# Decoder kernel, first attention stage: the key-partition scores of a group's four heads issued back to back in two ring places

## The reference

```
A0, causal self-attention, 16 heads of 16 values, 512 keys:
  q3, k3 = x @ wq, x @ wk                       # 3 numbers a head
  scores = (q3 . k3) * scale + (q3 . dir)(k3 . dir), masked above the diagonal
  out    = softmax(scores) @ v, then @ wo
X0, cross attention, 16 heads of 16, 1024 keys of the context:
  q = x @ Wq + bq; k, v = ctx @ Wk + bk, ctx @ Wv + bv
  out = softmax(clip(q . k / 4, +-10000)) @ v, then @ Wo + bo
```

## Time and profile before

| | us |
|---|---|
| median of 3 launches | 1334.27 (1333.01 to 1334.39) |
| the profiled execution, its own time | 1329.35 |
| its span, first to last instruction | 1327.6 |
| PE busy | 1193.6 (90%) |
| DVE busy | 742.4 (56%) |
| ACT busy | 556.9 (42%) |
| POOL busy | 89.6 (7%) |
| mean granted clock of TensorE | 0.956 of full speed |

### The profile page before, as it was taken

The page is one execution under the profiler, slowest core; times in us unless marked ns, Lnnn a source line. Parts: engine busy times, 40 slices in busy tenths (PEclk is TensorE's granted clock), DMA queues, the critical chain, the costliest instruction groups (busy, mean ns, idle before and its releaser), DMA issues.

```text
span 1327.6 us, 20645 instructions
## 1 busy us (share of the span) xinstructions
PE 1193.6 (90%) x7754; PEld 754.9 (57%) x7754; DVE 742.4 (56%) x1099; ACT 556.9 (42%) x1070; POOL 89.6 (7%) x127
## 2 busy tenths in 40 slices
PE   5999887899999986889599999999999999998887
PEld 3454444233332234778367777767777777777545
DVE  3346476888898845453256554655455554554322
ACT  1343332555555641221156663655334444453230
POOL 1112211000000003000000000000000000000120
PEclk9898877999999987999799999999999999999989
DMA  5010002000000002000242331223443333120000
GB/s 169 9 49 18 8 1 64 0 1 1 1 1 1 1 1 80 0 0 1 68 119 65 80 80 33 65 64 81 113 120 80 80 81 81 31 50 1 0 16 16
DMA packets 46917, 57.47 MB, mean 43 GB/s; under 512 B 12635, under 2 KB 25446, under 8 KB 46822
## 3 DMA queue, kind: packets, MB, share of 16 engines
q1 hardware_dynamic: 43062, 52.48, 16.3%
q10 hardware_dynamic: 3760, 3.67, 0.9%
HBM read 15.23 MB, written 3.15 MB: 14 GB/s over the span
## 4 chain that ended last, share of the span: by engine, by line
PE 79%; DVE 9%; issue 6%; ACT 3%; POOL 1%; DMA 1%; SPq 1%; POOLq 0%; ACTq 0%; DVEq 0%
PE p_unit L1531 21%; PE p_ring L1531 11%; PE p_ring L1632 9%; PE p_out L1655 8%; PE p_ring L1551 8%; PE p_ring L1598 7%; PE p_out L1621 6%; PE p_unit L1716 2%; PE p_ring L1576 2%; PE p_unit L1675 1%; DVE probT_b L1341 1%; PE p_ring L1590 1%; DVE stats L1244 1%; POOL m_z L1064 1%; PE p_ring L1569 1%
## 5 line engine op out<-in xcount | busy, mean ns | idle before, releaser
L1153 ACT ACTIVATE probT_b<-p_ring 128x512 f32<-128x512 f32 x144 | 84.5, 598 | 260.4 <-PE p_ring L1632 260.0
L1311 DVE TENSOR_REDUCE halves<-p_ring 128x2 f32<-128x1024 f32 x128 | 155.6, 1218 | 40.9 <-PE p_ring L1576 40.7
L1341 DVE COPY probT_b<-p_ring 128x512 f32<-128x512 f32 x112 | 77.4, 691 | 174.0 <-PE p_ring L1632 174.0
L1135 ACT ACTIVATE prob_a<-p_ring 128x1024 f32<-128x1024 f32 x128 | 130.7, 1023 | 93.8 <-PE p_ring L1598 93.8
L1293 DVE TENSOR_REDUCE nmax<-p_ring 128x2 f32<-128x1024 f32 (+1 forms) x128 | 155.9, 1218 | 23.5 <-PE p_ring L1551 23.5
L1121 ACT ACTIVATE prob_b<-p_ring,nmax 128x512 f32<-128x512 f32 (+1 forms) x192 | 158.7, 835 | 2.6 <-DVE nmax L1293 2.3
L1551 PE MATMUL p_ring<-stacks 128*128 128x512 f32 x512 | 150.8, 417 | 4.5 <-ACT prob_b L1121 4.5
L1632 PE MATMUL p_ring<-ident,prob_b 128*128 128x128 f32 x1024 | 134.6, 274 | 0.0
L1632 PEld LDWEIGHTS p_ring<-ident,prob_b 128*128 128x128 f32 x1024 | 115.8, 141 | 27.7 <-issue 25.8
L1598 PE MATMUL p_ring<-x_q,x_kq 32*128 32x512 f32 x512 | 126.5, 656 | 0.0
L1551 PEld LDWEIGHTS p_ring<-stacks 128*128 128x128 f32 x512 | 87.0, 190 | 17.0 <-ACT prob_b L1121 5.1
(11 more groups left out here) (201 smaller groups left out, 1658.6 us busy)
## 6 DMA issues: line engine op xcount, KB each, us to landing
stacks<-splitH_b SPq DMA_DIRECT2D x144, 128.0 KB, 2.4
stacks<-splitL_b SPq DMA_DIRECT2D x144, 128.0 KB, 2.4
a_st<-a_image SPq DMA_DIRECT2D x64, 32.0 KB, 1.8
ctx_raw<-in_ctx ACTq DMA_DIRECT2D x1, 1536.0 KB, 15.5
x<-in_x ACTq DMA_DIRECT2D x2, 512.0 KB, 5.2
k_words<-in_L_ffn_k SPq DMA_DIRECT2D x1, 1024.0 KB, 6.7
a_wq<-in_L_attn_Wq SPq DMA_DIRECT2D x1, 1024.0 KB, 6.2
a_wo<-in_L_attn_Wpost SPq DMA_DIRECT2D x1, 1024.0 KB, 9.3
```

What stands on the lines that cost most here:

```text
L1135: nc.scalar.activation(prob_place(key), slot_of("S2", key), ACT.Exp, accum_out=x0_sums[:, m:m + 1]).then_inc(done["E2"], 1)
L1311: nc.vector.tensor_reduce(to, src, AX.X, ALU.max, negate=True).then_inc(done["M1"], 1)
L1341: keep_turned(dve, key, lambda o, i: nc.vector.tensor_copy(o, i)).then_inc(done["VD"], 1)
```

## The change

`scored` is a new list of S2 items whose E2 is still to come. When it is empty and the next group's maxima are there, two S2 items (the two pairs of one block of keys, so all four heads) are added to the schedule at once, and both go into `scored`; in each iteration one E2 is taken from it. So the S2 of pair 1 is issued one iteration earlier, straight behind that of pair 0, and the ring's order becomes S2 S2 S1 S1 in place of S2 S1 S2 S1. Nothing else moves except what depends on it: the k and q units of X0 and the loads of A0's stacks wait for the last S2 of an earlier group, and come an iteration sooner. The remaining edits name the places of the operands by (batch, group) in place of a position in `PAIRS`; with `PAIRS` as it is they give the same places. The number of iterations and of instructions stays.

```diff
@@ paired_stream
-        if s < len(second) and age("UD", "mt", *second[s][:3]) >= 2:
-            it = second[s]
-            s += 1
-            sched.add("S2", *it)
+        if not scored and s < len(second) and age("UD", "mt", *second[s][:3]) >= 2:
+            for it in second[s:s + 2]:
+                sched.add("S2", *it)
+                scored.append(it)
+            s += 2
+        if scored:
+            it = scored.pop(0)
             sched.add("E2", *it)
             fresh.append(it)
@@ build_schedule
-    def used(n):
-        return [("S2", prob_items(PAIRS[n])[-1])] if n >= 0 else []
+    def used(L, n):
+        return [("S2", prob_items((L, n // 4, n % 4))[-1])] if n >= 0 else []
@@ block.tensor, "S1" of X0
-                        place = (G - 8) % HELD
+                        place = place_of_heads((L, b, g))
```

More of the change, by code:

```diff
@@ L153, in paired_stream @@
     heads = [list(c) for c in chains]
-    pending, owed, clean, adds, keep = [], [], [], [], []
+    pending, owed, clean, adds, keep, scored = [], [], [], [], [], []
     f = s = n = 0
@@ L170, in ready @@
         return item[0] <= n and all(a in sched.at for a in item[2])
-    while f < len(first) or s < len(second) or pending or owed or clean or adds or keep or any(heads):
+    while f < len(first) or s < len(second) or pending or owed or clean or adds or keep or scored or any(heads):
         while pending:
@@ L373, in a0_start @@
         for g in range(4):
-            out.append(step("DS", "A0", b, g, after=[UD("q", "A0", b)] + used(4 * b + g - HELD)))
+            out.append(step("DS", "A0", b, g, after=[UD("q", "A0", b)] + used("A0", 4 * b + g - HELD)))
         return out
@@ L381, in x0_keys @@
         n = 4 * b + g - HELD
-        return [unit("k", "X0", b, g, h, after=used(8 + n) if n >= 0 else []) for h in range(2)]
+        return [unit("k", "X0", b, g, h, after=used("X0", n)) for h in range(2)]
     def x0_queries(b, g):
         n = 4 * b + g - HELD
-        return [unit("q", "X0", b, g, after=[turned_x("A0", b)] + (used(8 + n) if n >= 0 else []))]
+        return [unit("q", "X0", b, g, after=[turned_x("A0", b)] + used("X0", n))]
     last_one = prob_items(PAIRS[-1])[-1]
@@ L773, in prob_place, with x0_back, place_of_heads @@
             return prob_a[:, prob_no[it] % NPT, :, :]
+        def x0_back(b, g):
+            n = 4 * b + g - HELD
+            return ("X0", n // 4, n % 4)
+        def place_of_heads(grp):
+            return (4 * grp[1] + grp[2]) % HELD
         def pair_back(grp, k):
@@ L950, in _ @@
                     if grp >= HELD:
-                        wait(sp, "S2", *prob_items(PAIRS[grp - HELD])[-1])
+                        wait(sp, "S2", *prob_items(("A0", (grp - HELD) // 4, (grp - HELD) % 4))[-1])
                     for which in range(2):
@@ L1036, in _ @@
                     if 4 * b + g >= HELD:
-                        wait(pool, "S1", *max_items(PAIRS[8 + 4 * b + g - HELD])[-1])
+                        wait(pool, "S1", *max_items(x0_back(b, g))[-1])
                     nc.gpsimd.tensor_copy(x0_kqF[:, place, part, :], x0_kq[:, place, part, :]).then_inc(done["KF"], 1)
@@ L1189, in _ @@
                         if 4 * b + g >= HELD:
-                            wait(act, "S2", *prob_items(PAIRS[8 + 4 * b + g - HELD])[-1])
+                            wait(act, "S2", *prob_items(x0_back(b, g))[-1])
                         if u[0] == "q":
@@ L1452, in _ @@
                             ins = nc.vector.tensor_tensor(a0_q2[:, G % 2, :], p_unit[:, :],
-                                                          a0_st[:, G % HELD, 1, :].bitcast(F32), ALU.add)
+                                                          a0_st[:, place_of_heads(grp), 1, :].bitcast(F32), ALU.add)
                         else:
                             ins = nc.vector.tensor_tensor(x0_q2[:, G % 2, :], p_unit[:, :],
-                                                          x0_kq[:, (G - 8) % HELD, 2, :], ALU.add)
+                                                          x0_kq[:, place_of_heads(grp), 2, :], ALU.add)
                     elif u[0] == "dt":
@@ L1560, in _ @@
                     if L == "A0":
-                        pe.wait_ge(a0_stacked[G % HELD], 16 * 8 * (G // HELD + 1))
+                        pe.wait_ge(a0_stacked[place_of_heads(key[:3])], 16 * 8 * ((4 * b + g) // HELD + 1))
                         w = 128 * (i + 1)
@@ L1564, in _ @@
                             r = 64 * pr + 32 * aa
-                            nc.tensor.matmul(o[:, aa, 0:w], a0_st[r:r + 17, G % HELD, 1, 128 * i:128 * i + 128],
-                                             a0_st[r:r + 17, G % HELD, 0, 0:w], start=True, stop=False,
+                            nc.tensor.matmul(o[:, aa, 0:w], a0_st[r:r + 17, place_of_heads(key[:3]), 1, 128 * i:128 * i + 128],
+                                             a0_st[r:r + 17, place_of_heads(key[:3]), 0, 0:w], start=True, stop=False,
                                              tile_position=(r, 0))
@@ L1590, in _ @@
                                 ins = nc.tensor.matmul(o[:, aa, at:at + T - 128 * c],
-                                                       a0_st[r:r + 17, G % HELD, 0, 128 * c:128 * c + 128],
+                                                       a0_st[r:r + 17, place_of_heads(key[:3]), 0, 128 * c:128 * c + 128],
                                                        a0_q2[r:r + 17, G % 2, 128 * c:T], start=True, stop=True,
```

## The result

The changed kernel takes 1351.91 us (median of 11 runs, 1339.91 to 1360.14), the kernel before in the same session 1333.01 us (11 runs, 1326.90 to 1338.54). The ratio is 1.0133 with a 95% interval of 1.0098 to 1.0167: slower by 13 to 22 us. Ratios are estimated over all launches but the slowest one of the changed kernel (1360.14), so a ratio can differ by some tenths of a per cent from the quotient of two medians, which is 1.0142 here. The forecast was 1344.7 in a range of 1334 to 1358, so the side and the range hold. The sizes of its terms don't.

What follows compares the result with a forecast made beforehand. TensorE held the chain for 79% of the span; PE and DVE were nearly full in X0, PE in A0. Terms 8.0 + 0.1 - 0.2 - 1.0 + 1.0 + 2.5 = 10.4 on the 1334.27 median gave 1344.7 us, range 1334 to 1358.

Steps and rivals of the forecast that it cites:

- the stall behind the q copy: X0 groups with units: ACT copies q ahead of the second E2, so PE idles 1.44 us before the next two S2.
- a change of more than 5 us ahead of 205 us: Sign named beforehand: a change this large in the trace there would show that the prediction has A0 wrong.
- A0, the step that failed: A0: copy stalls against 0.15 to 0.2 us saved per two S2; between minus 5 and plus 7, plus 1 taken.
- both S1 stand uncovered: X0 on PE: the two S1 cost 0.32 and 0.43 us; with 1.07 for two S2, 1.82 against 1.6 before.
- the wait of the first S1 for the M1 just before it: X0's new order: 1.88 us from M1 to M1 where it was 1.73, making 3.61 us per two S2.
- The clock: Five X0 stalls may halve PE's clock, costing 0 to 17 us; half the stalls at 1 us taken, plus 2.5.
- The rival of a falling clock: X0 stalls and iterations without units halve PE's clock: some 17 us instead of 2.5, 1359 us; chance 0.15.
- Number 1 to 7: X0 group, first to seventh M1, with k, k and q units: 16.8 us against 15.02, plus 1.8.
- Number 7 to 9 and 9 to 15: X0 group, seventh to ninth M1: 4.84 against 5.17, minus 0.3; ninth to fifteenth: 10.8 against 10.69, plus 0.1 to 0.2.
- The end of X0: Where no S1 is left, one S2 or PV is saved: minus 1.0 us, between minus 2 and 0.
- The sum: X0 8.0 + 0.1 - 0.2 - 1.0, A0 plus 1.0, clock plus 2.5: 10.4 us slower.
- Packing: Faster rival: X0's adjacent S2 save PE time, 9 us, 1325 us (chance 0.12); in full 27 us, 1307 us (0.03).

Runs made afterwards that it cites:

- A0 filled: Six more mask matmuls in every S1 of A0: added to the changed kernel 1346.0 us (1.0088), to the kernel before 1329.9 us (0.9994).
- taking it away alone: Kernel before with six more mask matmuls per A0 S1, and A0's two S1 pairs swapped, so S1 takes the preceding S2's rows: 1339.2 us (1.0050).
- taken away, in whole and in part: Changed kernel, S1 ahead of the two S2: 1360.7 us; changed kernel with six more mask matmuls per A0 S1, PV ahead of S1 in A0: 1344.1 us.
- copies behind E2: Changed kernel with ACT's copies of X0's k and q units behind the iteration's E2 instead of ahead of it: 1349.0 us (1.0103).
- couples in A0 only: Changed kernel issuing two S2 together only in A0, X0 one S2 an iteration as before: 1353.2 us (1.0163).
- couples and late copies in X0 only: Changed kernel with two S2 together only in X0, and ACT's copies of X0's k and q units behind E2: 1338.3 us (1.0022).
- couples in X0 only: Changed kernel issuing two S2 together only in X0, A0 as before: 1332.2 us (0.9991).

## Why the prediction came out as it did

That the change would cost, and that X0's groups would be longer by the stall behind the q copy, was right. That the total fell into the range was luck: X0 as a whole costs nothing, and A0, which was put at next to nothing, costs all of it. The prediction named the sign itself: a change of more than 5 us ahead of 205 us would show that it has A0 wrong, and X0 began 24.5 us late.

- **A0, the step that failed.** The prediction's sentence was that its "S2 is one pass and short, so PE gains little there", with bounds of minus 5 to plus 7 from copy stalls and a small gain a couple, and plus 1 taken. With A0 filled, X0 starts 11.1 us late (184.0 against 172.9), and 6.2 us of that is lost in five groups at full clock. Two terms stood in the working for X0 ("both S1 stand uncovered", and the wait of the first S1 for the M1 just before it), and neither was counted in A0. In X0 packing saves PE more than the uncovered S1 cost it: busy 158.8 us against 165.9 in the five groups, with DVE busy 85% of the time. In A0, where PE is busy 91% and DVE half of the time, PE's work grows, by 3.0 us in the five groups of the filled kernels, and 3.1 us of M1 waits come with it. That the lost cover costs is shown by taking it away alone. That the M1 waits cost is not: they were taken away, in whole and in part, and those groups stayed as long. What makes the rest of the 6.2 us stays open.
- **The clock.** I put it at plus 2.5 for stalls in X0. There it cost at most 0.7 us (one group of 36.6). It fell in A0, where the traced execution of the changed kernel was at half clock for 41 us on end from 103.9 us; with the filler the time is 5.9 us less by the medians, which is not clear of the noise. The rival of a falling clock had the wrong place: X0 is granted 0.99 from 276.1 to 456.3 us.
- **The stall behind the q copy.** Right: 1.35 us against 1.44, and every start from the first k unit to the second couple is within 0.1 us of the forecast, counted from the first S1 at 313.28, but for the S1 behind the first couple (6.58 against 7.05). It was not what sets the group, as the copies behind E2 show.
- **Number 1 to 7.** 16.08 us against 16.8. The first M1 comes 1.06 after its S1, not 0.61, since DVE is behind, which takes 0.45 off. The S1 behind the second couple starts inside it, so that M1 number 5 comes 13.58 after the first S1, not 13.82: 0.24. From number 5 to 7 it is 1.75 and 1.81, not 1.73 and 1.88: 0.05.
- **Number 7 to 9 and 9 to 15.** Minus 0.47 (forecast minus 0.3) and minus 0.03 (plus 0.1 to 0.2). A couple is 3.55 us, not 3.61, and was 3.56 before. So a group costs 0.57 instead of 1.6, and five such groups 2.9 instead of 8.0.
- **The end of X0.** Minus 2.7 (55.9 to 53.2) against minus 1.0, with bounds of minus 2 to 0: more than the bound. I counted one S2 or PV; which steps make the rest was not followed.
- **The sum.** X0 as run is near 0 where 6.9 was forecast (8.0, 0.1, minus 0.2, minus 1.0). A0 with its clock is 18.2 us by the medians (couples in A0 only, 1353.2 - 1335.0), 21.8 by the ratio and 24.5 by the trace, where 3.5 stood, the whole clock term counted in. The whole is 18.9 us by the medians, against 10.4.
- **Packing.** The eight records do run beside one another in 1.14 us. That rival missed for the reason given: half of the gain was taken before, because each S2 already had an S1 beside it. In A0 the cover that is lost and the couples together cost PE 3.0 us of work in five groups, where they save it 7.1 in five groups of X0.

## What to carry to other kernels

Before two matmuls are put side by side because they use different rows, count what each of them runs beside now; what loses its partner must be priced on the engine that bounds that stage, stage by stage, and not once for both. A new ring order shifts which read each item waits for, but the length of a wait in the trace is not its price: here two orders that took it away, in whole or in part, gained nothing there. To tell order from clock, run both orders with the same harmless filler and compare at equal granted clock.

## What the runs showed of the hardware

- The longest half-clock stretch of the changed kernel, with the stretch ahead of it, and then one of the kernel with couples and late copies in X0 only. TensorE's queue in its A0 is that of before; on ACT only the copies of X0's units stand later, near 60 us and behind 160 us, outside the stretch shown:

```profile
93.20:103.40 10.20, 9.12 (x68) 5.57 (x64) 3.74 (x6) 5.03 (x7) 1.63 (x4) 1.00 0.00 0
103.90:144.90 41.00, 40.03 (x216) 18.99 (x216) 19.68 (x27) 12.63 (x16) 7.10 (x14) 0.50 0.07 20
```

```profile
97.40:134.90 37.50, 37.14 (x215) 16.77 (x213) 21.52 (x30) 13.29 (x17) 7.28 (x15) 0.50 0.06 15
```

PE is busy 40.03 of 41.0 us at 0.50, after 9.12 of 10.2 at full clock, so the busy share does not tell the level. The last row's kernel too spends 37.5 us on end at half clock, with A0's old order on TensorE, so such a stretch is not tied to the new order. A0's fifth and sixth group, whose queues are the same, take 35.9 us there (104.1 to 140.0, clock 0.57) and 28.9 us in the kernel with couples in X0 only (102.8 to 131.7, clock 0.83): 7.0 us with no other difference than the clock. A0's second group, in the kernel before and in that with couples in X0 only, has the same queues too:

```profile
49.40:66.80 17.40, 16.39 (x88) 7.81 (x88) 7.24 (x10) 8.84 (x18) 3.37 (x7) 0.80 0.00 1
```

```profile
50.10:65.10 15.00, 13.88 (x88) 6.72 (x88) 7.21 (x10) 8.47 (x18) 3.36 (x7) 1.00 0.00 1
```

This is also the likely reason why the kernel before spreads over 1326 to 1343 us. In the launches beside the experiments (79 in all), the 18 under 1330 us had a mean clock of 0.949 to 0.957 and the 17 over 1338 us one of 0.937 to 0.950. No run set the clock by itself.

- 384 more full-array bf16 matmuls in A0 (six for each of 64 S1) cost the kernel before nothing that could be measured (0.9994, 0.9970 to 1.0018).
- A half-clock group costs far less than double: A0's group without units took 16.9 us in the changed kernel at half clock and 14.0 at full clock, although the latter was filled. In the old order it took 15.9 us at 0.50 (couples and late copies in X0) and 12.5 us filled at 1.00.
